# Two attentions and four inner layers on one Trainium2 core: drains left out, and the start of the inner layers reordered

## The reference, cut to what matters

```
xn = layernorm(x)
x  = x + attention(xn) * silu(ffn(xn))
```

```
h = shift_token(x);  q, k, v = split(h @ wqkv)        # 8 heads of 64
q, k = rotary_xpos(l2norm(q) * qs, l2norm(k) * ksc)   # cosines, sines, scales
x = x + local_attention(q, k, v) @ wo                 # windows of 64
h = layernorm(shift_token(x)) * lg + lb
a, g = split(h @ w1 + b1);  x = x + (a * gelu(g)) @ w2 + b2
```

## Time and profile before

| | us |
|---|---|
| runs (3), lowest / median / highest | 1752.48 / 1752.79 / 1757.74 |
| the profiled execution's own time | 1758.61 |
| its span, first to last instruction | 1756.5 |
| PE / PEld busy in the span | 1542.0 / 1183.8 |
| DVE / ACT / POOL busy in the span | 1327.8 / 1218.3 / 1099.6 |

### The profile page before, as it was taken

One profiled execution on the slowest core, in us unless ns is written; L12 is line 12 of the kernel. 1 busy time (PEld: TensorE's weight loads), 2 busy tenths in 40 slices (PEclk: granted clock), 3 DMA queues, 4 the chain that ended last, 5 costly groups with the idle time before them and its releaser, 6 DMA issues. The chain is left out here.

```text
span 1756.5 us, 44283 instructions
## 1 busy us (share of the span) xinstructions
PE 1542.0 (88%) x16972; PEld 1183.8 (67%) x16988; DVE 1327.8 (76%) x2187; ACT 1218.3 (69%) x2065; POOL 1099.6 (63%) x661
## 2 busy tenths in 40 slices
PE   6899996999999599999999569899999999999985
PEld 5577774666666366666666347777777777777774
DVE  4899984554555499999998488788888888888753
ACT  2577774444444478888888258888888888888863
POOL 1666762444444388888888367666777667777614
PEclk7899998999999789999999589999999999999997
DMA  5000000000000410000000001111111111111113
GB/s 170 2 3 3 3 3 15 8 15 7 7 7 1 151 30 2 14 2 14 2 13 11 12 16 29 25 26 26 26 26 26 26 26 26 26 26 26 26 26 102
DMA packets 56839, 44.14 MB, mean 25 GB/s; under 512 B 28152, under 2 KB 47900, under 8 KB 56388
## 3 DMA queue, kind: packets, MB, share of 16 engines
q1 hardware_dynamic: 56644, 41.45, 8.9%
HBM read 17.75 MB, written 4.23 MB: 13 GB/s over the span
## 5 line engine op out<-in xcount | busy, mean ns | idle before, releaser
L832 POOL TENSOR_TENSOR a_prob<-a_prob,a_top 128x1024 f32<-128x1024 f32 x128 | 239.8, 1895 | 58.5 <-DVE a_top L1023 58.4
L1235 POOL TENSOR_TENSOR e_hh<-e_h,e_hh 128x512 fp32r<-128x512 f32 x112 | 144.2, 1290 | 166.8 <-ACT e_hh L1219 165.4
L1494 POOL TENSOR_TENSOR i_qk<-i_qk,i_rt 128x1024 f32<-128x1024 f32 x64 | 152.1, 2376 | 46.5 <-DVE i_rt L1937 41.9
L1504 POOL TENSOR_TENSOR i_qk<-i_qk,i_rn 128x1024 f32<-128x1024 f32 x64 | 122.6, 1916 | 83.8 <-DVE i_rn L1916 83.8
L1256 DVE TENSOR_TENSOR e_h<-ps,e_sg 128x512 f32<-128x512 f32 x112 | 77.3, 690 | 123.9 <-PE ps L1118 104.3
L1793 ACT ACTIVATE i_prob<-i_prob,i_top 128x128 f32<-128x128 f32 x512 | 156.4, 391 | 16.1 <-DVE i_top L1925 14.2
L1202 ACT ACTIVATE e_sg<-ps 128x512 f32<-128x512 f32 x112 | 67.0, 598 | 141.4 <-PE ps L1118 141.4
L978 ACT ACTIVATE a_probT<-ps 128x1024 f32<-128x1024 f32 x128 | 131.1, 1024 | 45.3 <-PE ps L908 45.3
L1020 DVE TENSOR_TENSOR a_prob<-ps,a_table 128x1024 f32<-128x1024 f32 x128 | 148.6, 1203 | 13.7 <-PE ps L900 13.5
L1491 POOL TENSOR_TENSOR i_qk<-i_raw,i_rot 128x1024 f32<-128x1024 f32 x59 | 140.1, 2375 | 25.0 <-issue 25.0
L908 PEld LDWEIGHTS ps<-ident,a_prob 128*128 128x128 f32 x1024 | 113.4, 142 | 62.7 <-ACT a_probT L978 48.8
(11 more groups left out here) (305 smaller groups left out, 4390.5 us busy)
## 6 DMA issues: line engine op xcount, KB each, us to landing
i_V<-i_V SPq DMA_DIRECT2D x96, 130.0 KB, 2.3
a_table<-skew_scratch SPq DMA_DIRECT2D x2, 2048.0 KB, 12.6
X<-in_L_attn_x SPq DMA_DIRECT2D x4, 512.0 KB, 6.1
a_table<-in_c_l_table SPq DMA_DIRECT2D x1, 2048.0 KB, 8.3
e_xs<-Y SPq DMA_DIRECT2D x8, 256.0 KB, 2.3
i_ms<-Y SPq DMA_DIRECT2D x16, 128.0 KB, 2.4
i_ms<-Y SPq DMA_DIRECT2D x16, 112.0 KB, 2.4
out_dram<-X SPq DMA_DIRECT2D x7, 256.0 KB, 2.3
```

The lines of the kernel that those rows point to most:

```text
L832: nc.gpsimd.tensor_tensor(s, s, top[:, slot].unsqueeze(2).broadcast_to([P, HG, KW]), ALU.subtract).then_inc(shifted, 1)
L1235: nc.gpsimd.tensor_tensor(hh[0:n, b % HBUF, 1, :], h[0:n, b % HBUF, :], hh[0:n, b % HBUF, 0, :].bitcast(F32), ALU.subtract).then_inc(h_lo, 1)
L1494: nc.gpsimd.tensor_tensor(s, s, rt[:], ALU.add).then_inc(rotated, 1)
L1504: nc.gpsimd.tensor_tensor(flat, flat, rn[:, T // TPB % 2, T % TPB].unsqueeze(2).broadcast_to([P, 2 * FH, FD]), ALU.mult).then_inc(qk_done, 1)
```

## The change

Four things are changed. In both short-head attentions the drain between add and maximum is left out (also in the odd steps), and `row_max(n)` waits for `biased` instead; in the first one the drain behind `normalise` goes too. In the fill the projections of tiles 1 and 3 go to banks 6 and 7, those of 0, 2 and 4 to 0 and 1, and the wait of `project_qk(T)` becomes `fill_banks_free`: `qk_sb` and `sin_done` of tile T - 2, for T = 1 also `b1_done`; `sums(0)`, which uses the banks 6 and 7, waits for the readers of the fill. In the steps below 0 VectorE does `keep_token` ahead of `sines`. `low_weights(1)` moves from step FIRST + 4 to FIRST + 1, behind `add_shifts`, and ScalarE makes `w_hi` ahead of its table load.

```diff
--- before.py
+++ after.py
@@ -701,6 +701,7 @@
                 nc.vector.tensor_tensor(prob[:, slot].rearrange('p (b x) k -> p b x k', b=2), ps[:, 2 * (n % 2):2 * (n % 2) + 2, :].rearrange('p b (x k) -> p b x k', k=KW), heads[:, 2 * half:2 * half + 2, XX * pair:XX * (pair + 1), :], ALU.add).then_inc(biased, 1)
 
             def row_max(n, slot):
+                dve.wait_ge(biased, n + 1)
                 nc.vector.tensor_reduce(top[:, slot], prob[:, slot], AX.X, ALU.max).then_inc(max_done, 1)
 
             def normalise(T):
@@ -709,7 +710,6 @@
                 nc.vector.reciprocal(rden[:, :], ps[:, 6, P:2 * P])
                 dve.drain()
                 nc.vector.tensor_tensor(oT[:, T % 4, :], ps[:, 6, 0:P], rden[:, :], ALU.mult).then_inc(o_sb, 1)
-                dve.drain()
 
             def job(n, kind, i):
                 dve.wait_ge(aux_ps, n + 1)
@@ -1405,6 +1404,16 @@
                 eng.wait_ge(g_sb, R * NC + c + 1)
                 eng.wait_ge(a_sb, R * NC + c + 1)
 
+        def qk_bank(T):
+            return 6 if T in (1, 3) else 0
+
+        def fill_banks_free(eng, T):
+
+            if T == 1:
+                eng.wait_ge(b1_done, 1)
+            after(eng, qk_sb, T - 1)
+            after(eng, sin_done, T - 1)
+
         def bank_3_free(eng, step):
 
             after(eng, x_sb, max(0, min(step + LEAD + 1, TT)))
@@ -1555,9 +1564,10 @@
                 pe.wait_ge(x_sb, T + 1)
                 for j in range(2):
                     f = slice(j * INNER, (j + 1) * INNER)
-                    nc.tensor.matmul(ps[:, j, :], here(h_hi, T), w_hi[:, l, f], start=True, stop=False)
-                    nc.tensor.matmul(ps[:, j, :], here(h_hi, T), w_lo[:, l, f], start=False, stop=False)
-                    last = nc.tensor.matmul(ps[:, j, :], here(h_lo, T), w_hi[:, l, f], start=False, stop=True)
+                    out = ps[:, qk_bank(T) + j, :]
+                    nc.tensor.matmul(out, here(h_hi, T), w_hi[:, l, f], start=True, stop=False)
+                    nc.tensor.matmul(out, here(h_hi, T), w_lo[:, l, f], start=False, stop=False)
+                    last = nc.tensor.matmul(out, here(h_lo, T), w_hi[:, l, f], start=False, stop=True)
                 last.then_inc(qk_ps, 1)
 
             def project_v(T):
@@ -1611,7 +1621,9 @@
                     pe.wait_ge(v_next[T % VBUF // TPB], 16 * (T // VBUF + 1))
                 after(pe, oT_sb, T)
                 after(pe, o_sb, T)
-                pe.wait_ge(b1_done, 1)
+                if T == 0:
+                    pe.wait_ge(qk_sb, 4)
+                    pe.wait_ge(sin_done, 4)
                 R, c = round_at(T + 1, 8)
                 if R is not None and c == 0:
                     pe.wait_ge(m_norm, R + 1)
@@ -1690,7 +1702,10 @@
                     bank_3_free(pe, step)
                     score(step)
                 if is_tile(step + LEAD):
-                    banks_01_free(pe, step)
+                    if step < 0:
+                        fill_banks_free(pe, step + LEAD)
+                    else:
+                        banks_01_free(pe, step)
                     project_qk(step + LEAD)
                 if is_tile(step - 2):
                     transpose_out(step - 2)
@@ -1745,17 +1760,17 @@
                 act.add_instruction(mybir.InstLoadActFuncSet(act_func_set_id=LN_EXP_SET, name=nc.get_next_instruction_name(),
                                                              ins=[], outs=[]))
 
-            load_ln_exp()
             act.wait_ge(qkv_loaded, 16 * DEPTH)
             for l in range(DEPTH):
                 nc.scalar.activation(w_hi[:, l, :], wqkv[:, l, :], ACT.Copy).then_inc(hi_done, 1)
+            load_ln_exp()
             act.wait_ge(w_loaded, 16 * NLOAD)
 
             def keep_qk(T):
                 act.wait_ge(qk_ps, T + 1)
                 after(act, sin_done, T - 1)
                 after(act, cos_done, T - 1 - LEAD)
-                nc.scalar.activation(raw[:, T % 2].rearrange("p j h d -> p j (h d)"), ps[:, 0:2, :], ACT.Copy).then_inc(qk_sb, 1)
+                nc.scalar.activation(raw[:, T % 2].rearrange("p j h d -> p j (h d)"), ps[:, qk_bank(T):qk_bank(T) + 2, :], ACT.Copy).then_inc(qk_sb, 1)
 
             def squares(T):
                 after(act, ss_done, T)
@@ -1929,10 +1944,10 @@
                 if T < LEAD:
                     for j in range(2):
                         table = rot[:, layer(T), T % TPB, 2 * j, :].unsqueeze(1).broadcast_to([P, FH, FD])
-                        nc.vector.tensor_tensor(qk[:, T % QBUF, j], ps[:, j, :].rearrange("p (h d) -> p h d", h=FH), table, ALU.mult)
+                        nc.vector.tensor_tensor(qk[:, T % QBUF, j], ps[:, qk_bank(T) + j, :].rearrange("p (h d) -> p h d", h=FH), table, ALU.mult)
                 after(dve, rotated, T)
                 for j in range(2):
-                    src = ps[:, j, :].rearrange("p (h s d) -> p h s d", h=FH, s=2)[:, :, ::-1, :]
+                    src = ps[:, qk_bank(T) + j, :].rearrange("p (h s d) -> p h s d", h=FH, s=2)[:, :, ::-1, :]
                     table = rot[:, layer(T), T % TPB, 2 * j + 1, :].rearrange("p (s d) -> p s d", s=2)
                     last = nc.vector.tensor_tensor(rt[:, j].rearrange("p h (s d) -> p h s d", s=2), src,
                                                    table.unsqueeze(1).broadcast_to([P, FH, 2, HF]), ALU.mult)
@@ -2063,10 +2078,10 @@
                     rotation_table(0)
                     dve.drain()
                     add_shifts()
+                    low_weights(1)
                 if step in (1, 2):
                     low_w1(step - 1)
                 if step == FIRST + 4:
-                    low_weights(1)
                     rotation_table(1)
                 R, c = round_at(step, 8)
                 late = R is not None and c == 0 and is_tile(step)
@@ -2076,10 +2091,14 @@
                     square_sums(step + LEAD - 1)
                 if is_tile(step) and not late:
                     add_mask(step)
+                if step < 0:
+                    bank_3_written(step)
+                    keep_token(step + LEAD + 1)
                 if is_tile(step + LEAD):
                     sines(step + LEAD)
-                bank_3_written(step)
-                if is_tile(step + LEAD + 1):
+                if step >= 0:
+                    bank_3_written(step)
+                if step >= 0 and is_tile(step + LEAD + 1):
                     keep_token(step + LEAD + 1)
                 if is_tile(step - 2):
                     add_out(step - 2)
```

## The result

| | us |
|---|---|
| kernel before, median (4 runs) | 1752.63 (1750.58 to 1757.74) |
| changed kernel, median (4 runs) | 1729.94 (1726.67 to 1735.21) |
| ratio, 95% interval | 0.988 (0.9848 to 0.9911) |
| profiled execution of the changed kernel | 1728.87 (span 1726.8; before 1758.61, span 1756.5) |

The account below looks back on a forecast made before the run. It took TensorE to pace the window attention outside router bursts, TensorE and a GpSimd-ScalarE loop the bias attention, a serial chain the fill. 3.7 + 0.3 + 6.9 = 10.9 us off 1752.8 gave 1742 us, range 1733 to 1749.

Parts of the forecast that it names:

- window attention 3.7: Window attention: leaving out drains removes about 3.7 of TensorE's 7.2 us of waits for VectorE's oT.
- fill 6.9: Start of the inner layers: alternating banks, earlier tokens and moved weights gain 6.9 us, ends 4 and 9.
- bias attention 0.3: Bias attention: fewer drains gain only 0.3 us, at the start, before TensorE has work.
- The 64 tiles: Inner layers from the fifth square sums to the last mask add: no gain of their own, 0 us.
- the two longer, earlier ones keep their stall less about 0.5 each: Window attention: TensorE's stalls behind the two longer, earlier router bursts of VectorE shrink by about 0.5 us each.
- The end of 7.2: Window attention: upper end of the drains' gain, all 7.2 us of TensorE's waits for oT gone.
- the wait on `biased` at no cost: Window attention: the added semaphore wait ahead of the maxima costs nothing, at most 5.8 us on 64 pairs.
- Rival (b): Both attentions: the drains give nothing, so the 3.7 and 0.3 us go; 1746 us, chance 0.13.
- the end of 16: Bias attention: upper end of the drains' gain, the 16 us that TensorE idles there.
- The hand-back: Fill: 1.5 of the 8.4 us gained by projection 3 are lost again by the fifth square sums.
- Rival (c): Fill: its gain is given back because what follows waits for something set otherwise; 1749 us, chance 0.10.
- The steady state behind it starts that much earlier, from the same place of each queue: Inner layers behind the fill: they start earlier by the fill's 6.9 us and otherwise run as before.

Follow-up runs that it names:

- e7: The changed kernel with the search for the second largest in the first router burst made twice, same values; 1738.29 us (one run).
- e2: The kernel before with only the window attention's drains changed, all else as before; 1740.34 us, ratio 0.9947 to before.
- e4: The kernel before with only the fill's changes, but every projection written to banks 0 and 1; 1748.11 us (one run).
- e6: The kernel before with only the fill's changes, alternating banks kept but the token copy behind the sines again; 1748.24 us (one run).
- e5: The kernel before with only the fill's changes, but `low_weights(1)` back at step FIRST + 4; 1740.85 us (one run).
- f2: The changed kernel with 64 drains added to VectorE's queue ahead of the bias attention; 1726.32 us, ratio 0.9889 to before.
- c2: The changed kernel, unchanged, run and profiled again; 1728.64 us, ratio 0.9889 to before.
- g2: The changed kernel with 128 drains added to VectorE's queue ahead of the bias attention; 1733.67 us, ratio 0.9904 to before.
- e1: The kernel before with only the fill's changes, both attentions as before; 1737.65 us, ratio 0.9929 to before.

## Why the prediction was wrong

- **The sum.** It named the right parts and missed three sizes, all in one direction: window attention 3.7, measured 7.1 to 7.6; fill 6.9, measured 8.2; bias attention 0.3, measured 1 to 2. The 64 tiles were forecast at nothing and are 5.7 shorter in the four profiles. That makes 12 of the 14 us by which the profiles (25.0) lie above the sum (10.9); the rest is in stages that nobody touched. The medians lie 9 to 12 above it; how much of that the 64 tiles carry stays open.
- **The step that failed most: "the two longer, earlier ones keep their stall less about 0.5 each".** The longest went from 3.3 to 1.2. I took the burst as of fixed length; one operation in it was held 1.54 us by GpSimd, and an earlier VectorE got ahead of that (nine profiles against nine). I had used the same mechanism for the fill and did not look for it in the burst. The Trainium skill, SBUF — State Buffer, section "SBUF: two separate sides", says that whichever of the two starts first gets the pair for the whole instruction; the rows agree: GpSimd at 74.93 held VectorE's 75.14, while in the changed kernel the same instruction ran its 0.43 us.
- **The clock behind a stall was left out.** The sum counted stalls at their own length. Before, 3.4 us at half clock followed the stall, about 1.7 us; e7 shows 2.7 us of cost beside 5.9 of waits. The end of 7.2 that I gave for this term was thus no bound.
- **Window attention otherwise**: the VectorE tile of 5.74, TensorE's pace (scores at 207.89 and 220.84, 12.95 for two tiles) and the wait on `biased` at no cost were right. Rival (b) falls with e2: 9 us come from drains. The Trainium skill, VectorE: DVE Perf Modes, section "The DRAIN you can't avoid", says that the next operation does not start until the pipe is empty, by which the drains gain nothing. It adds that an operation which is not held starts earlier, and that is what the rows show: 79.31 lies before 77.06 + 2.33.
- **Bias attention**: right that GpSimd and not VectorE decides (10.2 us of waits, unchanged). The 1 to 2 us lie above my 0.3 and far under the end of 16.
- **Fill**: the chain, its pace, the held norms and table came as forecast. The hand-back was too large, 1.5 against 0.5 (8.7 us gained at projection 3, 8.2 at the fifth square sums): counted from the start of the inner layers, projection 3 came 0.4 us earlier than I had it, projection 4 1.1 and the fifth square sums 1.3; each small term was taken a little too long. e4 and e6 confirm that both the banks and the order are needed, e5 the weights' 1.8. Rival (c), the fill given back, does not hold: the fifth square sums and all behind them moved up. What I held against it was misread: not all inputs are loaded before 977 us, the mask and the rotary tables land at 979.6 and 980.5, ahead of their first use.
- **The steady state was taken as untouched.** "The steady state behind it starts that much earlier, from the same place of each queue": of semaphores this was true, of VectorE's instruction stream it was not: the gaps of 0.40 us fall ahead of other instructions.

## What to carry to other kernels

Price a stall by its length and by what TensorE's clock does behind it, and look in several traces at what the clock did after stalls of that size: it need not be the same each time. Before costing a burst as fixed, see whether GpSimd held one of its operations: shifting the engine by half a microsecond can free or catch it. And when a change shortens one engine's instruction stream, compare stages that it doesn't touch, in several profiles; a difference there need not be the change's merit, and the median of runs may not show it.

## What the runs showed of the hardware that was not expected

- VectorE's stream has a gap of 0.40 us ahead of every 128th record in all 20 profiles, hidden where it waits anyhow; what makes it is not shown. Adding 64 drains moved the gaps to other instructions, adding 128 put them back ahead of the same ones. 64 drains took 3 of the 8.4 idle us there, 128 took 5.5 (ratios 0.9889 in f2, as in c2, and 0.9904 in g2).
- At the same place of the program, TensorE went on at full clock after an idle time of 1.66 or 1.67 us in 13 profiles and fell to half clock after one of 2.02 to 2.04 in seven; yet in e1 and e5 it went on at full clock after a stall of 3.25 us in the window attention.
- GpSimd holds also the smallest VectorE operations with two SBUF inputs: 2.21 us for 128x32 elements that take 0.19.
